# Splitting one early weight load over two issuing queues, at the start of a one-core FFN kernel

## What is computed

```python
base = einsum('btd,od->bto', x, W)
logits = einsum('btd,ed->bte', x, Wr) + 5.0 * one_hot(ids)
gates = top-2 softmax of logits
h = einsum('btd,erd->bter', x, A)
cond = base + 2.0 * einsum('bter,bte,eor->bto', h, gates, B)
out = x + einsum('bti,oi->bto', cond, U * S @ V.T)
```

## Time and profile before

| what | value |
|---|---|
| median of 3 runs | 154.18 us (153.75 to 154.49) |
| the profiled execution's own time | 154.44 us |
| its span, first to last instruction | 152.7 us |
| mean granted TensorE clock | 0.995 |
| TensorE busy | 147.4 us (97%) |
| VectorE, ScalarE, GpSimd busy | 107.2, 63.5, 72.3 us |
| bytes moved | 32.72 MB, mean 214 GB/s |

### The profile page before, as it was taken

The page is one execution under the profiler, slowest core; times in us unless marked ns, Lnnn a source line. Parts: engine busy times, 40 slices in busy tenths (PEclk is TensorE's granted clock), DMA queues, the critical chain, the costliest instruction groups (busy, mean ns, idle before and its releaser), DMA issues.

```text
span 152.7 us, 2912 instructions
## 1 busy us (share of the span) xinstructions
PE 147.4 (97%) x1056; PEld 139.1 (91%) x1056; DVE 107.2 (70%) x297; ACT 63.5 (42%) x141; POOL 72.3 (47%) x57
## 2 busy tenths in 40 slices
PE   7799999999999999999999999999999999999991
PEld 5699999999999989998999899989999998998880
DVE  0488887759478999978765875587558736795851
ACT  4397876894546422446014612351334105013000
POOL 2000242993560659292966186636655640721700
PEclk9999999999999999999999999999999999999998
DMA  5999999999303030049719903980591068006184
GB/s 171 315 400 409 400 405 411 410 407 409 132 6 137 0 137 4 0 192 345 288 60 350 386 34 136 338 347 10 211 286 57 0 277 262 17 0 275 69 339 142
DMA packets 10670, 32.72 MB, mean 214 GB/s; under 512 B 1441, under 2 KB 1953, under 8 KB 10529
## 3 DMA queue, kind: packets, MB, share of 16 engines
q1 hardware_dynamic: 10368, 31.96, 55.8%
q10 hardware_dynamic: 288, 0.59, 1.2%
HBM read 24.16 MB, written 8.39 MB: 213 GB/s over the span
## 4 chain that ended last, share of the span: by engine, by line
PE 93%; DMA 3%; ACT 0%; DVE 0%; SPq 0%; issue 0%; DVEq 0%
PE fin L343 13%; PE fin L345 13%; PE fin L344 13%; PE pj L344 10%; PE pj L343 10%; PE pj L345 10%; PE zt L343 6%; PE zt L345 6%; PE zt L344 6%; DMA w_raw<-in_W 3%; PE gt L447 1%; PE zt L434 1%; PE fin L380 1%; PE gt L344 1%; PE gt L345 1%; PE fin L390 1%
## 5 line engine op out<-in xcount | busy, mean ns | idle before, releaser
L281 POOL TENSOR_TENSOR xT_lo<-xt_raw,xT_hi 128x1024 fp32r<-128x1024 f32 x15 | 36.5, 2443 | 25.2 <-DVE gh L801 7.9
L304 POOL TENSOR_TENSOR x_all<-x_all,vw_raw 128x512 f32<-128x512 f32 x21 | 26.6, 1297 | 25.8 <-DVE vw_raw L849 25.8
L343 PE MATMUL pj<-proj_hi,xT_hi 128*128 128x264 f32 x128 | 36.9, 288 | 0.0
L344 PE MATMUL pj<-proj_lo,xT_hi 128*128 128x264 f32 x128 | 36.3, 284 | 0.0
L345 PE MATMUL pj<-proj_hi,xT_lo 128*128 128x264 f32 x128 | 36.2, 283 | 0.0
L343 PE MATMUL fin<-v_hi,w_hi 128*128 128x256 f32 (+1 forms) x80 | 25.7, 321 | 0.0
L344 PE MATMUL fin<-v_lo,w_hi 128*128 128x256 f32 (+1 forms) x80 | 25.6, 320 | 0.0
L345 PE MATMUL fin<-v_hi,w_lo 128*128 128x256 f32 (+1 forms) x80 | 25.6, 320 | 0.0
L344 PEld LDWEIGHTS pj<-proj_lo,xT_hi 128*128 128x128 f32 x128 | 24.1, 189 | 0.2
L343 PEld LDWEIGHTS pj<-proj_hi,xT_hi 128*128 128x128 f32 x128 | 24.1, 188 | 0.2
L345 PEld LDWEIGHTS pj<-proj_hi,xT_lo 128*128 128x128 f32 x128 | 24.0, 188 | 0.0
(11 more groups left out here) (100 smaller groups left out, 282.5 us busy)
## 6 DMA issues: line engine op xcount, KB each, us to landing
xt_raw<-in_xt SPq DMA_DIRECT2D x16, 512.0 KB, 7.6
x_all<-in_x SPq DMA_DIRECT2D x16, 512.0 KB, 6.5
out<-x_all SPq DMA_DIRECT2D x13, 512.0 KB, 3.2
vw_raw<-in_VW SPq DMA_DIRECT2D x6, 384.0 KB, 7.1
w_raw<-in_W SPq DMA_DIRECT2D x8, 256.0 KB, 6.6
out<-x_all SPq DMA_DIRECT2D x5, 256.0 KB, 2.0
w_raw<-in_U SPq DMA_DIRECT2D x1, 1024.0 KB, 8.8
aw_raw<-in_AW SPq DMA_DIRECT2D x1, 544.0 KB, 7.2
```

Of the source, the lines that this page charges most:

```text
L281: nc.gpsimd.tensor_sub(xT_lo[:, t % XTR, :, :], xt_raw[:, t % XTR, :, :], xT_hi[:, t % XTR, :, :].bitcast(F32)).then_inc(xt_lo, 1)
L304: nc.gpsimd.tensor_add(x_all[:, t % XR, cols], x_all[:, t % XR, cols], ups[:, j, :]).then_inc(side_add, 1)
L343: nc.tensor.matmul(dst, l_hi, r_hi, start=first, stop=False, skip_group_check=shared)
L344: nc.tensor.matmul(dst, l_hi, r_lo, start=False, stop=False, skip_group_check=shared)
```

## The change

W0 was one transfer of 128 rows on SP's queue. It becomes two of 64 rows (128 KB each): rows 0 to 63 from SP, in the same place, and rows 64 to 127 from ACT, between the second part of VW0 and VW1. Both add 16 to the same semaphore, so ScalarE's cast of half chunk 1 now waits for 32. VW1 becomes the third transfer of ACT's queue.

```diff
             first = RANK + P
             sp.dma_start(vw_raw[:, 0, 0:first], VW[0, :, 0:first]).then_inc(vw_load[0], 16)
-            load_w(0)
+            sp.dma_start(w_raw[0:P // 2, 0, :], W[0, 0:P // 2, :]).then_inc(w_load[0], 16)
             load_w(1)
...
                 if h == 1:
-                    act.wait_ge(w_load[k], 16)
+                    act.wait_ge(w_load[k], 32 if k == 0 else 16)
...
             act.dma_start(vw_raw[:, 0, first:], VW[0, :, first:]).then_inc(vw_rest_load, 16)
+            act.dma_start(w_raw[P // 2:P, 0, :], W[0, P // 2:P, :]).then_inc(w_load[0], 16)
             act.dma_start(vw_raw[:, 1, :], VW[1, :, :]).then_inc(vw_load[1], 16)
```

## The result

The changed kernel takes 155.59 us (median of 15 executions, 154.48 to 158.21), the kernel before 154.14 (153.47 to 154.66). The ratio is 1.0092, with a 95% interval of 1.0071 to 1.0113. The forecast was 154.6 with a range up to 155.4, so it is right in direction and too small: 1.45 us slower, not 0.4. Two of the 15 executions (157.02 and 158.21, mean granted clock 0.989 and 0.985) are left out of the ratio, and so are, further down, one of 157.87 in tiny_between and one of 515.33 in before_ids_first.

What follows compares the result with a forecast made beforehand. TensorE, busy without a gap from 8.60 us, was taken as the bound, so VW1's 0.4 us delay reaches the end: 154.44 + 0.4 = 154.84, less 0.26 for the profiled execution's excess over the median, forecast 154.6, range 153.5 to 155.4.

Steps and rivals of the forecast that it cites:

- What bounds the kernel: TensorE is busy from 8.60 to 147 us, so any shift of half chunk 2's start at 8.60 reaches the end.
- the tie at 8.59: Half chunk 2's two conditions, TensorE free (through W0) and w_hi ready (through VW1), are both met at 8.59 us.
- W0 0.6 us earlier: W0 in halves lands at 5.5 instead of 6.13 us; half chunk 1 starts at 6.3 and ends at 7.97.
- VW1 0.4 us later: VW1 behind half of W0 lands at 7.86 instead of 7.46 us; half chunk 2 starts at 9.00 instead of 8.60.
- equal-share rule: DMA engines take turns between queues with work; by it VW1 would land 0.55 to 0.6 us later.
- The wait for 32: ScalarE's wait before casting half chunk 1 stays at the same instruction and adds none; no cost.
- SP: SP's queue issues as many transfers at the same moments as before; no cost.
- ScalarE's extra issue: Table load and warming move by 0.46 us; half chunk 0 may slip 0.05 us; cost 0.
- Nothing moves: Rival: a tail sets VW1's landing, near 7.46 to 7.6 us as before; 153.9 to 154.3 us, chance 0.28.
- the tail goes: Rival: the split cures VW1's late last share, gaining 0.63 to 0.88 us; 153.3 to 153.6 us, chance 0.10.
- VW1 suffers more than its bytes: Rival: VW1's tail stretches with what lies ahead, costing 1.0 to 1.4 us; 155.0 to 155.6 us, chance 0.15.
- The clock: Rival: the hole before half chunk 2 lowers TensorE's clock, costing 3 us more; 157 us, chance 0.03.

Runs made afterwards that it cites:

- tiny_between: Kernel before, with an unread 4 KB transfer added on ScalarE's queue between the second part of VW0 and VW1: 156.07 us, ratio 1.0128.
- before_ids_first: Kernel before, with SyncE's 8 KB ids transfer moved ahead of W1: 154.20 us, ratio 1.0004.
- column_split: Changed kernel, with W0 split by columns (128 rows of 1 KB from each queue) instead of rows: 155.75 us, ratio 1.0134.
- swap_queues: Kernel before, with the two second transfers exchanged, VW1 from SyncE and whole W0 from ScalarE: 154.00 us, ratio 1.0016.
- delay_both: Kernel before, with VW1's issue waiting for a GpSimd constant (1.72 us) and the ids transfer moved ahead of W1: 153.90 us, ratio 1.0004.
- column_ids: Changed kernel, with W0 split by columns instead of rows and the ids transfer moved ahead of W1: 154.25 us, ratio 1.0038.
- pure_delay: Kernel before, with VW1's issue waiting for a GpSimd constant (1.71 us instead of 1.16), no transfer added or split: 155.00 us, ratio 1.0056.
- after_ids_first: Changed kernel, with SyncE's 8 KB ids transfer moved ahead of W1, so W1 is issued after VW1: 155.44 us, ratio 1.0098.
- vw1_on_pool: Changed kernel, with VW1 issued by GpSimd instead of ScalarE: 156.75 us, ratio 1.0172.
- both_on_sp: Changed kernel, with both halves of W0 issued by SyncE and ScalarE issuing as in the kernel before: 154.41 us, ratio 1.0043.
- half_third: Changed kernel, with ScalarE's second and third transfers exchanged, VW1 ahead of its half of W0: 154.98 us, ratio 1.0074.
- late_issue: Kernel before, with VW1's issue written behind ScalarE's warming instruction (went out at 1.92 us): 155.32 us, ratio 1.0124.

## Why the prediction was right or wrong

*What bounds the kernel* held for everything behind 8.60 and for the two conditions on it. The chain named W0, and W0 alone was a false lead: column_split and tiny_between had its cast run at 4.6 and ran 1.3% slower. What it left out is the third condition, half chunk 0 itself: with both W0 and VW1 early, in swap_queues, delay_both and column_ids, half chunk 2 started at 7.70 to 8.11 in the profiles, right behind what stood before it. And the tie at 8.59 belongs to one execution of the kernel before; its median execution starts at about 8.0, by the estimate from the spans. Looking for the second condition on 8.60, VW1, gave the right sign, the right place (before the second group of L380) and the law that its delay is the kernel's.

*W0 0.6 us earlier* was wrong. It landed at 6.6 instead of 5.5, for ScalarE's half took 5.4 us. Its cast ran at 4.5 in delay_both, without any halving and with VW1 issued 0.55 us later, and at 4.6 in column_split. In neither does it pay, as half chunk 0 itself ends at 6.8 to 6.9.

*VW1 0.4 us later* is the step that failed, by size: 7.46 to 8.86, 1.40 us. ScalarE's second cast of v_hi came at 8.88, outside the 7.7 to 8.3 that the prediction named. The mechanism named, W1 and VW2 served beside VW1 where W0 was before, is borne out in kind: a later issue beside an unmoved W1 is enough for a loss (pure_delay), and with W1 moved back that loss is gone (delay_both). It is not the whole of it: in the changed kernel the same move of W1 left the loss (after_ids_first, 1.0098). Three things made the term small. First, it counted only the bytes, and its middle value of 0.4 leaned on VW1 landing at 7.63 as the last of the four transfers; in the profile it landed behind W1 (1.76 + 5.8 = 7.6, as forecast) by another 1.3 us. Second, it called the later issue free "as long as its queue is still busy". pure_delay delays it by 0.55 us and changes nothing else, and its median is 1.1 us higher. Third, it took one issue as 0.46 us, and in the row form they took 0.54 and 0.85. How the 1.40 us divide among these isn't shown. The equal-share rule of the Trainium skill ("DMA: Bandwidth & Descriptors", "Queues, rings and completion order") would have given 0.55 to 0.6 and misses too, though between 3.5 and 6.5 us of the changed kernel both queues did move about equal parts (0.16 and 0.16 MB, then 0.25 and 0.22).

*The wait for 32* and *SP* cost nothing by themselves, as said. *ScalarE's extra issue* was put at 0.05 us for half chunk 0; the cast slipped from 3.60 to 4.16 and half chunk 0 ended at 6.99 instead of 6.05. That was hidden behind VW1, as TensorE was free 0.97 us before it was needed.

*The rivals.* "Nothing moves" and "the tail goes" are out, with VW1 at 8.86. Column_ids met the conditions of the second, VW1 before 6.7 and W0 before 5.4, and its profiled execution did start at 7.70 and take 153.47; its median was still 154.25, and the kernel before reaches such a start by itself (7.5 by the estimate, at 153.27). "VW1 suffers more than its bytes" is what happened, at 0.15, and its price of 1.0 to 1.4 us (155.0 to 155.6) holds the measured median. The price doesn't follow from its reason, though: at half the mean rate 0.84 us become 1.68, and 154.18 + 1.0 is 155.2. So it was right with some luck, and no run shows a share at half rate. The clock did not fall in the profiled execution (1.00 in every window of it to 147 us), but in vw1_on_pool it did, during a hole of 2.36 us; after the 2.18 us of tiny_between it was 1.00.

Why the last share of a transfer is late stays open. In the kernel before, 21 packets of ScalarE's queue were left after 5 us; in column_split 22 after 6.8. In swap_queues, both_on_sp and half_third the landing of the same 384 KB took 4.1, 3.9 and 4.0 us, which leaves no room for such a tail. The trace shows packets by queue and not by DMA engine, so what holds these few back isn't seen, nor why ScalarE's half of W0 landed 2.0 us after SyncE's in the changed kernel. And whether VW1's place is set by its order with W1 or by how long W1 stays away is open too: before_ids_first speaks for the second, after_ids_first fits neither.

No version beats the kernel before. In the profiles of delay_both (1.0004) and swap_queues (1.0016) both W0 and VW1 are in time, and TensorE works without a hole from half chunk 0 on; then the landing of VW0 and the early rate of matmuls bound the start.

## What to carry to other kernels

When the chain names one transfer, look for the next one that the same engine needs and compare their slack before splitting the first: here the two were level to 0.01 us in the profiled execution, the change and half_third only handed the wait from one to the other, and where both came early a third bound stood behind them. Don't take a later issue as free because its queue is busy: 0.55 us of delay cost 0.56% here, and an extra issue ahead of VW1 cost about 1% whether it carried 128 KB or 4. Test such a case with a pure delay and with the delay undone on the other side; that shows that bytes aren't needed for the loss. Then undo it in the changed kernel itself, which here did not help. And before explaining a profile, see where its execution stands among the others: the kernel before spreads over 1.5 us at its start by itself.

## What the runs showed of the hardware

- A 4 KB transfer between two others of ScalarE cost 1.28% (1.00 to 1.57), no less than 128 KB in its place (0.92%, 0.71 to 1.13).
- The same 384 KB, issued at 1.16 to 1.18 us, landed at 7.5 with W1 issued at 1.63 (before), at 5.2 with W1 at 1.76 (half_third) and at 5.6 with W1 at 2.11 (before_ids_first), one execution each.
- Among the issues of the first 2.5 us, one of 64 rows took 0.53 to 0.58 us where one of 128 rows took 0.33 to 0.46, and one of 128 rows right behind it 0.57 to 0.59 (SyncE) and 0.59 or 0.85 (ScalarE). In the column form with half the bytes in each of 128 rows they took 0.42 to 0.46.
- A transfer that is written behind an activation in ScalarE's list went out at 1.92 us while the table load was still running (late_issue).
- The first matmuls run at nearly half rate (groups of four start 0.85 us apart and not 0.48) for a time that differs between executions, while the clock row says 1.00 (in before_ids_first in every us from 4 to 8). There half chunk 0's three groups took:

```profile
4.20 1.42 PE L359 MATMUL fin<-v_hi,w_hi 128*128 128x256 f32 x4
5.42 1.05 PE L364 MATMUL fin<-v_lo,w_hi 128*128 128x256 f32 x4
6.28 1.05 PE L369 MATMUL fin<-v_hi,w_lo 128*128 128x256 f32 x4
```

L370's group took 0.64 in the earlier trace rows. This, with a start 0.06 us later, ends half chunk 0 at 7.33 and not at 6.05, more than any transfer edit brought half chunk 2 forward in a profile (0.9 us at most).
